# A five-layer graph network on one core: engine orders from a repeating table, and from a plan laid out operation by operation

## What is computed

```python
h = relu(layernorm(x));  x = x + gcn(h)          # weighted scatter over edges + degree term * h
h = relu(layernorm(x));  x = x + sage2(sage1(h)) # relu(mean(h[src]) @ Wl.T + b + h @ Wr.T), twice
h = relu(layernorm(x));  x = x + mlp(h)          # edge MLP, mean per dst, update MLP, residual, layernorm
h = relu(layernorm(x));  x = x + mean(h)         # relu(h @ Wself.T + b + mean_neighbours @ Wn.T + b)
```

## Time and profile before

| | us |
|---|---|
| median of three runs | 5694.75 |
| the profiled execution | 5692.87 |
| its span, first to last instruction | 5691.1 |
| PE busy | 4138.9 (73%) |
| DVE busy | 4096.6 (72%) |
| POOL busy | 3905.2 (69%) |
| ACT busy | 3611.1 (63%) |
| DMA moved | 892.93 MB, mean 157 GB/s |
| mean granted clock of PE | 0.860 |

### The profile page before, as it was taken

The page is one execution under the profiler, slowest core; times in us unless marked ns, Lnnn a source line. Parts: engine busy times, 40 slices in busy tenths (PEclk is TensorE's granted clock), DMA queues, the critical chain, the costliest instruction groups (busy, mean ns, idle before and its releaser), DMA issues. The chain is left out here.

```text
span 5691.1 us, 87559 instructions
## 1 busy us (share of the span) xinstructions
PE 4138.9 (73%) x24852; PEld 3234.2 (57%) x24852; DVE 4096.6 (72%) x19892; ACT 3611.1 (63%) x8952; POOL 3905.2 (69%) x3227
## 2 busy tenths in 40 slices
PE   6427777776677776988876888888698888455555
PEld 4316565555455555777755666666476676344444
DVE  7538888885899884766656777777498887455655
ACT  0027777786788775877765676666498887344444
POOL 6767777761677774777745677775477775577776
PEclk9758999998788887999978999999799999677777
DMA  9935766764566664666645878787455554333332
GB/s 231 321 111 152 193 189 188 195 178 144 126 162 160 154 139 97 160 139 142 141 104 172 226 204 246 202 251 185 125 142 122 131 132 94 100 116 111 112 113 67
DMA packets 906492, 892.93 MB, mean 157 GB/s; under 512 B 132770, under 2 KB 686124, under 8 KB 905938
## 3 DMA queue, kind: packets, MB, share of 16 engines
q1 hardware_dynamic: 561544, 589.64, 32.0%
q0 software_dynamic: 224000, 235.91, 23.9%
q10 hardware_dynamic: 120460, 61.78, 4.2%
HBM read 359.33 MB, written 533.69 MB: 157 GB/s over the span
## 5 line engine op out<-in xcount | busy, mean ns | idle before, releaser
L1049 POOL DMA_INDIRECT node<-sage_comb,leadd x400 | 653.8, 1635 | 304.2 <-DMA node<-sage_comb,leadd 162.3
L1049 POOL DMA_INDIRECT sums<-mean_comb,leads x200 | 330.7, 1654 | 178.3 <-DMA sums<-mean_comb,leads 65.0
L1049 POOL DMA_INDIRECT sums<-mlp_same,leadd x200 | 324.6, 1623 | 182.4 <-DMA sums<-mlp_same,leadd 68.3
L1049 POOL DMA_INDIRECT node<-gcn_comb,leads x200 | 327.5, 1637 | 132.5 <-DMA node<-gcn_comb,leads 62.2
L488 POOL DMA_INDIRECT sage_agg<-node,gidx x200 | 211.1, 1055 | 147.7 <-POOLq L784 82.6
L362 PE MATMUL gcn_p<-ident,gcn_dh 128*128 128x128 f32 x792 | 132.5, 298 | 247.0 <-ACT gcn_dh L356 246.9
L488 POOL DMA_INDIRECT xs<-in_x,gidx x200 | 234.9, 1175 | 86.6 <-issue 60.6
L488 POOL DMA_INDIRECT mlp_a<-node,gidx x200 | 201.8, 1009 | 125.7 <-issue 54.9
L362 PE MATMUL sage_p<-ident,sage_dh 128*128 128x128 f32 x924 | 162.6, 306 | 147.6 <-ACT sage_dh L356 145.8
L369 PE MATMUL sage_p<-wT,sage_dhT 128*128 128x128 f32 x1232 | 245.4, 324 | 32.2 <-ACT sage_dhT L917 17.7
L488 POOL DMA_INDIRECT sage_a<-node,gidx x200 | 203.0, 1015 | 94.6 <-issue 58.5
(11 more groups left out here) (359 smaller groups left out, 16424.1 us busy)
## 6 DMA issues: line engine op xcount, KB each, us to landing
node<-b SPq DMA_DIRECT2D x400, 256.0 KB
sums<-zero_row SPq DMA_DIRECT2D x400, 256.0 KB
node<-zero_row ACTq DMA_DIRECT2D x50, 1152.0 KB, 15.1
sage_dx<-in_x SPq DMA_DIRECT2D x77, 256.0 KB, 4.5
out<-sage_dy SPq DMA_DIRECT2D x77, 256.0 KB, 4.3
gcn_dx<-in_x SPq DMA_DIRECT2D x66, 256.0 KB, 4.7
out<-gcn_dy SPq DMA_DIRECT2D x66, 256.0 KB, 4.9
x_src<-xs SPq DMA_DIRECT2D x50, 256.0 KB, 5.7
```

What stands on the lines that cost most here:

```text
L1049: pool.indirect_dma_start(table, bass.IndirectOffsetOnAxis(ap=leads[:, i * G + c, t:t + 1], axis=0), e.comb[c][:, t, :], None, element_off ...
```

## The change

Nothing of what an operation does is changed. Three things are.

First, dense rows are shared out as 6, 4, 4, 2 and 3 streams, with 11 rounds in gcn and 10 in the others: 66 + 40 + 40 + 20 + 30 = 196 chunks in place of 66 + 33 + 44 + 22 + 33 = 198. Sage1's four dense streams share three PSUM banks.

Second, the order is no longer a repeated sequence. `Plan` now lays out every single operation of every round. It keeps a clock per engine, takes the operation that could begin first by the assumed lengths and handoff times, and among those of its engine that could begin within 100 ns of that takes the one with the smallest value `round * period + table value`. `order` is the list of all (name, round, stream) in the sequence chosen. The table values are now such weights, some negative.

Third, the lengths, which now enter the order, have new values throughout.

```diff
-ND = RD + 1
-SLOTS = {"gcn": range(0, 6), "sage1": range(6, 9), "sage2": range(9, 13), "mlp": range(13, 15), "mean": range(15, 18)}
+DENSE = {"gcn": (11,) * 6, "sage1": (10,) * 4, "sage2": (10,) * 4, "mlp": (10,) * 2, "mean": (10,) * 3}
+PARTS = [rounds for stage in DENSE.values() for rounds in stage]
...
-    "gcn": (8968, (
-        (7828, 7899, 7980, 7529, 8141, 8143, 7794, 8384, 14488, 16046, 16490, 17464, 19420, 8102, 8699, 9533, 9534,
+    "gcn": (218240, (
+        (213163, 185710, 603106, 167484, 249542, 300997, 248055, 207321, 155008, 338657, 201126, 104517, 303100,
...
+HANDOFF = {VECTOR: 120, SCALAR: 130, TENSOR: 200, GPSIMD: 2300, SYNC: 2300}
+LANDED = 2800
+PATIENCE = 100
...
+        while True:
+            able = []
+            for line in every:
+                if line.next < line.many and line.ready is not None:
+                    n = line.node
+                    begin = max(line.ready, free[n.eng])
+                    if n.take in held:
+                        ps, gives, pi = held[n.take]
+                        if pi >= len(gives.end):
+                            continue
+                        begin = max(begin, gives.end[pi] + HANDOFF[gives.node.eng])
+                    if n.adds in chain:
+                        begin = max(begin, chain[n.adds][3])
+                    able.append((begin, line))
+            if not able:
+                break
+            at, first = min(able, key=lambda a: (a[0], a[1].s, a[1].j))
+            begin, line = min((a for a in able if a[1].node.eng == first.node.eng and a[0] <= at + PATIENCE),
+                              key=lambda a: (a[1].next * period + a[1].when, a[1].s, a[1].j))
+            n, i = line.node, line.next
+            free[n.eng] = begin + n.length
...
 def rounds(step, plan):
-    for k in range(ND + plan.late):
-        for _, late, s, name in plan.items:
-            if 0 <= k - late < (RD if s < G else ND):
-                step(name, k - late, s)
+    for name, i, s in plan.order:
+        step(name, i, s)
...
-        dn = Dense(sb, sem, k, "sage1", every[5:8], False, TENSOR)
+        dn = Dense(sb, sem, k, "sage1", every[5:8], True, TENSOR)
...
-FETCH = 2500
-ADD = 3720
+FETCH = 2600
+ADD = 3800
```

More of the change, by code:

```diff
@@ L243, in holder @@
-    def holder(self, s, name, i):
-        while True:
-            s, name, gives, back = self.before[s, name]
-            i = i - back
-            if 0 <= i < (RD if s < G else ND):
-                return s, gives, i
-            if i < -self.late - 2:
-                return None
+            pairs = sum(1 for n in nodes if n.name.startswith("fetch"))
+            own = {}
+            for j, n in enumerate(nodes):
+                early = any(m.startswith("fetch") and back == 1 for m, back, lag in n.after)
+                release = 5000 + (s + 1) * pairs * 2600 if early else 4000 + 500 * s
+                own[n.name] = Line(s, j, n, many[s] - (1 if n.name.startswith(AHEAD) and s < G else 0), release, when[s][j])
@@ L1043, in add_pair @@
     pool.wait_ge(e.done[c], e.at.after(i, "keep"))
[L1044 removed]
+    held = plan.prior.get((c, name, i))
     if held is not None:
@@ L1128, in _ @@
             sp.wait_ge(e.filled, NCH * len(FILL) * 16)
-            for d in range(len(dn.slots)):
-                dense_sync(sp, dn, inp, out, "end", RD, d)
+            for d in range(len(dn.many)):
+                dense_sync(sp, dn, inp, out, "end", dn.many[d], d)
         @block.gpsimd
```

207 lines of the change are left out of this document (114 added, 93 removed), and 325 rows, old and new, of the table TIMES.

## The result

The changed kernel took 5471.76 us (median of four executions, 5462.52 to 5481.13), the kernel before, on the same chip, 5687.02 us (four, the three given above and one of 5679.3). The ratio is 0.9626, with a 95% interval of 0.9591 to 0.966: faster by 3.7%, where I had forecast 2.0%. The profiled execution took 5481.13 us, with a span of 5479.2.

A forecast was written before the change was run, and what follows sets the result against it. POOL was taken to pace gcn, sage2 and mlp, DVE sage1. Gcn -81, sage1 +40, sage2 -5, mlp -50, mean -15, final 0 sum to -111 us on 5692.87; forecast 5583 us, range 5480 to 5705.

The forecast's parts named there:

- What bounds gcn: Gcn: POOL sets the pace; dense work spread beside it takes the stage from 1069 to 988 us, -81 us.
- POOL's instructions beside a busier DVE: Gcn: POOL's adds lengthen a little as DVE gets denser, 2 us, inside the 18 us allowance.
- Sage1: Sage1 stage: DVE bounds it, seven more dense chunks add 66 us of DVE; +40 us (+27 to +78).
- Sage2: Sage2 stage: POOL paces; more add waits against a shorter tail and steadier fetches; -5 us (-25 to +35).
- the forecast's +18: Sage2: extra landing waits from POOL's adds standing closer and a longer closing run, +18 us.
- Mean: Mean stage: three dense chunks fewer give -35, POOL's add waits +20; -15 us (-60 to +40).
- Mlp: Mlp stage: POOL paces; landing waits -30, waits for ACT and DVE and the end -20; -50 us.
- rival A: Whole kernel: more is won, the order also takes POOL's waits for other engines; 5500 us, chance 0.15.
- Setup: Setup before the six stages: untouched at 357 us, a term of 0.
- Final: Final stage: no dense part, POOL's work and issue stay; 0 us (-40 to +30).
- B: Whole kernel: a wash, late operations block those behind them in an engine's list; 5690 us, chance 0.15.
- C: Whole kernel: slower, POOL's back-to-back adds wait 4.5 us each, not 2.5; 5780 us in mild form, chance 0.10.

The follow-up runs named there:

- e10: Changed kernel with the gcn stage alone back in the old repeated order, chip without pauses: 5591.21 us, ratio 0.9839 to the kernel before.
- e9: Changed kernel with the mlp stage alone back in the old repeated order, new dense shares kept, chip without pauses: 5583.68 us, ratio 0.9826 to the kernel before.
- e12: Changed kernel with only the first 30% of mlp's operations in the new order, the rest in the old, chip with pauses: 6418.69 us, ratio 1.0174.
- e14: Changed kernel with the first and last 30% of mlp's operations in the new order, the middle in the old, chip with pauses: 6411.63 us, ratio 1.0149.
- e11: Changed kernel, unchanged, run again on a chip with pauses: 6312.98 us, ratio 1.0006 to the kernel before.
- e1: Kernel before the change, unchanged, run again on a chip with pauses: 6305.36 us.
- e15: Changed kernel, unchanged, run again on a chip with pauses: 6310.58 us in one execution, beside 6326.34 for the kernel before.

## Why the prediction missed

The direction, the place and the signs of the large terms were right, and the forecast of 5583 us was 111 us too long: the measured 5471.76 lies 8 us below its range of 5480 to 5705. Step by step:

*What bounds gcn* was right. POOL's busy time, its issue and its landing waits are 738.93 + 178 + 37.5 = 955 us, and the stage is these with about 19 for its two ends. The long stop of the earlier trace rows is gone, as forecast. The 14 us by which -95 beats -81 are a difference of sizes. The closing run cost 15 waits of 3.1 us, 46 and not 52. The 18 us that I added because two engines near their limit don't mesh were not needed. POOL's own work came to 909 us in place of 903, and the two ends to about 19 in place of 15. e10 shows the mechanism by itself.

*POOL's instructions beside a busier DVE.* An add took 1652 ns in gcn after the change and 1637 before, with DVE busy 85% of the stage in place of 80%: 15 ns over 200 adds, 3 us; with the gathers POOL's busy time grew by 7 us (732.03 to 738.93), where I had allowed 2. The rule of the Trainium skill (SBUF — State Buffer, section "SBUF: two separate sides") that VectorE and GpSimd lock each other out of a shared port pair would have spoken against the change only if the adds or gathers had grown by much. The trace leaves it at most these 7 us of the stage's 974. Which of DVE's operations here take such a lock no run shows.

*Sage1* was right, with its reason: +38.8 for +40, DVE busy 728.63 us where the sum had 728, and POOL now waits for DVE's `sage_x` 87.9 us. In mid-stage DVE is busy 55.55 of 60 us, 93% for the 94% of the earlier trace rows.

*Sage2* gave -9.5 for -5, with POOL's landing waits at 86.1 us, where the forecast's +18 would have made 109 of the 91.0 in the earlier trace rows. The 13 places with two adds in a row outside the closing run did not cost their 2.5 us each on top: outside that run the waits are some 48 us, for 56.8 before.

*Mean* came to +1.5 for -15. The landing waits rose from 65.0 to 92.1 us as forecast (about 90), and the idle stretch of POOL at the end fell from 33.9 to 15.0. What did not come is the 35 us for three chunks fewer: DVE was busy 27 us less (655.22 to 627.87) and the stage did not get shorter by it.

*Mlp is the step that failed*: "-20 of the 104 us that POOL waits for ACT and DVE and of the 14.2 at the end". The end gave 4 us (14.2 to 10.2). Of the 104 us went 93: 103.7 before, 82.6 in e9 (the chunks: -21), 10.7 after (the order: -72). The other half of the term was right: -30 for the landing waits, measured 68.3 to 37.6. I held the waits for other engines to be the price of a chain that starts empty, which rival A said as well ("many sit at a stage's start, where a chunk's chain has nothing before it"). The trace of before could have told more. This is POOL's wait for DVE in the first 281 us of its mlp stage, and its wait for ACT in the last 277:

```profile
POOL mlp_a L488 <- DVE mlp_v L1668: 37.1, 5, 12.3
...
POOL sums L1049 <- ACT mlp_same L1072: 37.8, 4, 19.5
```

These two alone are 75 of the 104 us, and they lie at the two ends, where a repeated sequence has operations of the steady state left out and nothing put in their place. POOL waits five times for an `mlp_v`, between 3030 and 3151 us; I would expect one such wait from an empty chain alone, and one is what is left, 9.1 us. e9 shows that the order took these waits away: with the old order they are back at the same place (36.6 us in five waits in its first 276 us). Of the waits for ACT at the end it has 18.6 us, so the two chunks fewer had taken the other half. Why the repeated order has them, the empty places above, is argued from where they lay and from their number; the runs that should have shown it (e12 to e14) did not.

*Setup* was "untouched" at 357 us, a term of 0. The profiled execution had 335.4; e9 and e10, whose setup is the same code, had 356.9 and 356.8. So the 23 us are not a saving of the change as far as these three profiles tell. In the fast one DVE waits 91.3 us for PE's instruction queue, in the others 117 to 118, and POOL's 200 gathers take 1001 ns each in place of 1172 to 1175. Which comes first is open. With 357 us of setup the profiled execution would have taken some 5503 us, an estimate, and e9 and e10 less what their one stage costs come to 5500 and 5497; that is inside the range. So it takes the setup's 23 us, which no step foresaw, to put the time outside; mlp's 65 us are the largest part of the way to the range's end. The other three executions of the changed kernel were 7 to 19 us shorter than this one, so it is not a lucky one that made the gain look large.

*Final* was -10 for 0, inside its bounds.

The sum again, with what was measured: -95 + 39 - 9.5 - 115 + 1.5 - 10 - 23 = -212 us. Of the 101 us beyond the forecast's -111 mlp has 65, the setup 23, gcn 14, final 10 and sage2 5, and mean takes back 16; the rest of the 111 us is that the profiled execution took 9 us more than the median. Rival A ("more is won", 5500 us, chance 0.15) came closest, with its mlp at -90. B is excluded on this chip by the time itself, and by gcn and mlp, which won more than forecast; on the chips with pauses the outcome was B's (ratios 0.9987 and 1.0006), and POOL's long waits for `mlp_v` in e11 look like its mechanism, which no run shows by itself. C is excluded by the landing waits, which rose in no stage by more than 27 us. Its condition of 3.5 us a wait did not hold: the waits average 3.1 us in gcn, 2.5 in sage1, 2.7 in sage2, 2.4 in mean.

## What to carry to other kernels

Before pricing a new order, split each stage's waits of the pacing engine by place: a handful of waits at a stage's ends, several in a row for the same tile, may belong to the order and can go nearly as a whole, as they did in mlp. Look at the pacing engine's stop where a stage ends: work that the plan leaves behind the last of its work is paid nearly in full (stops of 82.57 us in gcn before, 48.3 us for an eleventh round in mlp). A fitted order is one piece with its table, its landing time and its number of rounds: changing any one of them alone cost 0.7% to 10% beside the changed kernel, on chips with pauses, so such an experiment doesn't price the part. And a gain from tight ordering can hang on the timing: 3.7% on one chip was nothing on chips where the engines paused.

## What the runs showed of the hardware

Three of the four chips numbered in the runs of this study held PE and DVE still again and again in the setup, in the kernel before and after alike: six times, 45 us apart, in e1 and e15, first for 26 and 33 us and then for 41 to 42 us (DVE). Between two of these stops DVE carried out 16 instructions and PE 16 matmuls, each time. POOL's indirect DMAs went on at one in 1.29 us meanwhile, and even took a bit less (975 to 982 ns each, for 1001 to 1175 on the chips without pauses). In the stages the stops hit DVE, ACT and PE, at no such even distance. The kernel before took 6217 to 6330 us there, 9% to 11% more than its 5687. Of this the setup has 130 us, gcn 162 and final 231 (e1 against the profile before), the other stages 9 to 39 each. The profile names no releaser for most of these pauses ("issue" or "remote"), and their cause is open.
